# Row maxima of self-attention as pairs of 64-row products, and scores in two single PSUM banks

## The chip, the cores and the metric

One NeuronCore of a Trainium2 (trn2) chip. The metric is the device time of one execution in microseconds, the median of several runs. PE is TensorE's matmul side, PEld its weight loads, DVE VectorE, ACT ScalarE, POOL GpSimd, SP the engine that issues most DMAs.

## What is computed

x is (2, 1024, 256). It is layer-normed and put through a conditioned transformer block; the result is added to x and goes through a quantised feed-forward. Cut to what matters here:

```python
h1 = adaln(x, t, norm1_w, norm1_b)
x = mha(h1, h1, attn1_wq, ...) + x          # 16 heads of 64, 1024 keys
h2 = adaln(x, t, norm2_w, norm2_b)
x = mha(h2, context, attn2_wq, ...) + x     # 77 keys
x = glu_ff(adaln(x, t, norm3_w, norm3_b), ...) + x
# mha: scores = q @ k.T / 8 ; attn = softmax(scores) ; out = attn @ v ; out @ wo + bo
```

The change is in the softmax of mha: its row maxima and its scores.

## The kernel before

**Units.** Self-attention runs over 16 units: 2 batches x 8 pairs of heads. In each unit both heads get q, k and v (items of PE that ACT and DVE split into a high and a low f16 part), maxima, scores, exps, the exps' low parts ("rest"), values, and two transposes of the result ("out"). Pieces of later work fill in: in units 0 to 3 the norms of the second batch, in units 4 to 7 and 12 to 15 two tiles of an output projection ("projA"), in units 8 to 11 two others and norms ("projB", "norm").

**Operands.** SP's `restack` copies q and k by DMA into `head_operands` (`HB`): per head four planes QS, QM, KH, KL of 128 rows. Rows 0 to 63 of QS hold the high part of q and rows 64 to 127 its low part; KH holds the high part of k in both halves.

**Maxima.** softmax needs the row maximum of the scores before the exps, because exps are taken of scores laid out with keys on the partitions; there the negated maximum comes in as one row of the product (row 64 of QM). A "max" item is one product of 128 rows, (q high + q low) x k high, 128 queries by 512 keys, one bank. There are 32 a unit (head, 8 query tiles, 2 halves of the keys), 512 in all. They alternate between the two banks of `mixed` (`M_[0]`, `M_[1]`). DVE reduces each (L1842), and after the last of a head reduces the pairs into `neg_max` (L1854); PE transposes that ("row", L870), ACT copies it and issues the DMA that puts it into row 64.

**Scores, exps, rest, values.** A unit has 16 chunks: head, half of the queries, group of 256 keys. A chunk of scores is four products of 512 columns (L904, L905, twice) into `scores{c % 2}`, a pair of banks; ACT takes one exp of 128 x 1024 (L1248); POOL (DVE for chunk 14) makes the low parts (L1574, L1869); values are 24 small products (L927 to L929) into `PV_[0]`. `exps` is a ring of four chunks. q, k, v, out, projections and norms take the bank `PV_[1]` in turn: each waits until ACT and DVE have emptied it.

**Order.** The order of a unit is written out by hand (FIRST_UNIT, SELF_UNIT; the last unit by a generic loop, `unit`). PE runs it as it stands; ACT, POOL and DVE run the same list with small shifts by kind (SELF_LAGS). Every engine works strictly in its order, so a wait holds all that stands behind it. The tail of SELF_UNIT before is

```python
("max", 1, 1, 5), ("values", 15), ("max", 1, 1, 6), ("max", 1, 1, 7), ("slot", 15), ("out", 0, 1), ("slot", 16)
```

The first number of a max, q, k, v, row or out says whether it is of this unit (0) or the next (1); "slot" marks only places for rare notes. In a unit the maxima of head 1 end early and those of the next unit's head 0 and half of its head 1 follow.

## Time and profile before

| | us |
|---|---|
| median of 3 runs | 1193.1 (1189.34 to 1197.38) |
| the profiled execution | 1193.03 |
| its span, first to last instruction | 1191.2 |
| PE busy | 1101.7 |
| DVE busy | 859.7 |
| POOL busy | 694.4 |
| ACT busy | 591.2 |

The span begins with the first instruction and ends with the last; 1.8 us of the execution lie outside. Self-attention runs from about 50 to 790 us, cross-attention to about 1000, the feed-forward to the end. A busy time is the sum of the listed durations with overlaps counted once. A view of waits says for whom an engine stood idle; the chain follows the work that ended last back in time.

### The profile page before, as it was taken

The numbers are of one execution on the slowest core, as the hardware profiler recorded it, in microseconds if no ns is written. First come the engines' busy times: TensorE is split into PE (matmuls) and PEld (weight loads), VectorE is DVE, ScalarE is ACT, GpSimd is POOL, SyncE is SP. The second block draws the span as 40 slices with busy tenths as digits, with TensorE's granted clock in tenths as the row PEclk, the third lists the DMA queues.
The fourth block names the chain that finished last, engine by engine and source line by source line (L and its number), as shares of the span: only waits on it lengthen the run. The fifth ranks groups of instructions, "written<-read, shape, count | busy, mean of one in ns | idle before, by whom it ended". The sixth has DMA issues, their size and how long they took to land.

```text
span 1191.2 us, 30646 instructions
## 1 busy us (share of the span) xinstructions
PE 1101.7 (92%) x12733; PEld 720.2 (60%) x12740; DVE 859.7 (72%) x1686; ACT 591.2 (50%) x856; POOL 694.4 (58%) x641
## 2 busy tenths in 40 slices
PE   4799999999999999999999999889899989999995
PEld 1355665665656656657656566567667666656663
DVE  6687767756657668678676676848867976887887
ACT  4444455444444444444444445544444544258668
POOL 5757766765656657777676556436534743533333
PEclk9899999999999999999999999999999999999999
DMA  8420220220220211202202203122432444000001
GB/s 288 118 61 2 55 55 1 55 55 2 55 54 2 55 28 28 55 2 55 55 2 55 54 2 90 37 59 59 131 85 60 87 103 152 1 1 10 10 18 36
DMA packets 41854, 63.52 MB, mean 53 GB/s; under 512 B 11459, under 2 KB 22383, under 8 KB 41461
## 3 DMA queue, kind: packets, MB, share of 16 engines
q1 hardware_dynamic: 40413, 60.91, 20.4%
q8 instruction: 101, 1.65, 0.6%
q10 hardware_dynamic: 1304, 0.66, 0.2%
q14 instruction: 36, 0.29, 0.1%
HBM read 20.63 MB, written 2.10 MB: 19 GB/s over the span
## 4 chain that ended last, share of the span: by engine, by line
PE 68%; DVE 16%; ACT 5%; DMA 4%; issue 4%; POOL 2%; SPq 0%; ACTq 0%; DVEq 0%
PE outs L839 9%; PE scores L904 8%; PE scores L905 7%; PE mixed L860 6%; PE outs L816 6%; PE scores L966 5%; PE outs L929 4%; PE outs L927 4%; DVE maxes L1842 4%; PE outs L928 4%; PE outs L980 4%; PE outs L849 3%; DMA head_operands<-neg_max_rows 3%; DVE exps_rest L1869 2%; PE outs L877 2%
## 5 line engine op out<-in xcount | busy, mean ns | idle before, releaser
L1574 POOL TENSOR_TENSOR exps_rest<-exps 128x1024 f16<-128x1024 f32 (+1 forms) x297 | 510.8, 1725 | 305.8 <-ACT exps L1248 304.8
L1248 ACT ACTIVATE exps<-scores 128x1024 f32<-128x1024 f32 (+1 forms) x320 | 297.1, 938 | 261.9 <-PE scores L905 242.1
L1842 DVE TENSOR_REDUCE maxes<-mixed 128x1 f32<-128x512 f32 x512 | 334.6, 683 | 90.9 <-PE mixed L860 86.4
L927 PE MATMUL outs<-values,exps 128*128 128x65 f16 (+1 forms) x2176 | 226.7, 193 | 1.8 <-POOL exps_rest L1574 1.7
L928 PE MATMUL outs<-values,exps 128*128 128x64 f16 (+1 forms) x2176 | 226.7, 192 | 0.0
L929 PE MATMUL outs<-values,exps_rest 128*128 128x65 f16 (+1 forms) x2176 | 226.4, 194 | 0.0
L904 PE MATMUL scores<-head_operands 128*128 128x512 f16 (+1 forms) x576 | 218.6, 380 | 6.9 <-DMA head_operands<-neg_max_rows 6.6
L905 PE MATMUL scores<-head_operands 128*128 128x512 f16 (+1 forms) x576 | 218.5, 379 | 0.0
L927 PEld LDWEIGHTS outs<-values,exps 128*128 128x128 bf16 (+1 forms) x2176 | 201.6, 98 | 22.3 <-POOL exps_rest L1574 3.4
L928 PEld LDWEIGHTS outs<-values,exps 128*128 128x128 bf16 (+1 forms) x2176 | 200.6, 98 | 23.4
L929 PEld LDWEIGHTS outs<-values,exps_rest 128*128 128x128 f16 (+1 forms) x2176 | 200.5, 97 | 0.0
L860 PE MATMUL mixed<-head_operands 128*128 128x512 f16 x512 | 178.0, 385 | 16.9 <-DVE maxes L1842 10.0
L839 PE MATMUL outs<-hT,weights 128*128 128x512 f16 x492 | 120.7, 382 | 3.4 <-DVE qk_pairs L1827 2.4
L1827 DVE SCALAR_TENSOR_TENSOR qk_pairs<-outs,qk_pairs 128x512 f16<-128x512 f32 x82 | 56.4, 688 | 77.7 <-ACT qk_pairs L1213 77.7
L860 PEld LDWEIGHTS mixed<-head_operands 128*128 128x128 f16 x512 | 48.7, 97 | 76.4 <-DVE maxes L1842 34.8
L816 PE MATMUL outs<-weights,attn_outT 128*128 128x256 f16 x744 | 92.0, 274 | 0.0
L904 PEld LDWEIGHTS scores<-head_operands 128*128 128x128 f16 (+1 forms) x576 | 57.4, 100 | 49.4 <-issue 8.8
L905 PEld LDWEIGHTS scores<-head_operands 128*128 128x128 f16 (+1 forms) x576 | 57.6, 100 | 49.0
L966 PE MATMUL scores<-hT,weights 128*128 128x512 f16 x384 | 86.8, 379 | 0.0
L1213 ACT ACTIVATE qk_pairs<-outs 128x512 f16<-128x512 f32 x82 | 49.0, 597 | 68.2 <-PE outs L839 66.6
L816 PEld LDWEIGHTS outs<-weights,attn_outT 128*128 128x128 f16 x744 | 71.4, 98 | 11.2
L839 PEld LDWEIGHTS outs<-hT,weights 128*128 128x128 f16 x492 | 43.9, 98 | 54.7 <-DVE attn_outT L1862 7.8
(204 smaller groups left out, 1576.9 us busy)
## 6 DMA issues: line engine op xcount, KB each, us to landing
head_operands<-qk_pairs SPq DMA_DIRECT2D x128, 256.0 KB, 4.4
head_operands<-qk_pairs SPq DMA_DIRECT2D x32, 128.0 KB, 2.4
stage<-in_L_xcond_ff_w_dram SPq DMA_DIRECT2D x3, 1024.0 KB, 5.0
residual<-in_x_dram SPq DMA_DIRECT2D x4, 512.0 KB, 10.0
stage<-in_L_ffn_w_dram SPq DMA_DIRECT2D x2, 1024.0 KB, 5.0
head_operands<-in_x_dram SPq DMA_DIRECT2D x1, 2048.0 KB, 9.4
out_dram<-out_tile SPq DMA_DIRECT2D x16, 128.0 KB, 1.7
attn_outT<-in_L_xcond_attn_wq_dram SPq DMA_DIRECT2D x1, 1024.0 KB, 8.6
```

Source lines behind the costliest of these rows:

```text
L816: last = mm(ITEM[bank][:, 0:D], OT[:, c, xh, t * P:(t + 1) * P], W[:, 3, wh, c * D:(c + 1) * D], start=(n_ == 0 and c == 4 * half), stop=( ...
L839: last = mm(m[:, 0:rhs.shape[-1]], W[:, 0 if kind == "q" else 1, wh, wc[c]], rhs, start=(n_ == 0 and c == 0), stop=(n_ == 2 and c == KC - 1))
L860: last = mm(m[:, :], hb[:, QS, t * P:(t + 1) * P], hb[:, KH, kh * HALF:(kh + 1) * HALF], start=True, stop=True)
L904: mm(o, kb[:, KH, :], hb[:, QS, :], start=True, stop=False)
L905: last = mm(o, kb[:, KL, :], hb[:, QM, :], start=False, stop=True)
L927: mm(o, eb[:, sl], vb[:, DH:VW], start=(kt == 0 and q == 0), stop=False, skip_group_check=True)
L928: mm(o[:, 0:DH], eb[:, sl], vb[:, 0:DH], start=False, stop=False, skip_group_check=True)
L929: last = mm(o, R[0:a.ks, slot, sl], vb[:, DH:VW], start=False, stop=(kt == a.kt - 1), skip_group_check=True)
L966: last = mm(SP_[f % 2][:, half * HALF:(half + 1) * HALF], WU[:, wh, k, half * F + f * P:half * F + (f + 1) * P], hT[:, xh, k, tc * HALF:(t ...
L1248: A(E[0:a.ks, c % RING, 0:n], SP_[c % 2][0:a.ks, 0:n], ACT.Exp, scale=SCALE).then_inc(s.exps, 1)
L1574: G.tensor_tensor(R[0:a.ks, c % RING, 0:n], e, e.bitcast(BF16).rearrange("p (n two) -> p n two", two=2)[:, :, 1], ALU.subtract).then_inc(s ...
L1842: V.tensor_reduce(mx[:, h, t, kh:kh + 1], m[:, :], AX_X, ALU.max).then_inc(s.maxed, 1)
```

## The change

Maxima. A max item now covers one query tile and all 1024 keys as two products of 64 rows each: high q by high k, keys 0 to 511 from rows 0 to 63 of the array, keys 512 to 1023 from rows 64 to 127. For the second, a new tile `query_copies` (QD) holds the high part of q in rows 64 to 127; a fourth DMA of `restack` fills it, behind a wait of SP for the maxima of the previous unit's same head. The item fills two banks: even tiles both banks of `mixed`, odd tiles both banks of `scores1`. The written orders always name two items together, a visit of four products into four banks. DVE reduces 128 x 1024 at once and straight into the negated maximum, so `maxes` and L1854 go. There are 16 items, 8 visits, a unit. (The low part of q no longer enters the maximum, which only has to lie near the true one.)

Scores. `scores0` alone is left: a chunk becomes two parts ("scores", 2c + j) with one bank and one exp of 128 x 512 each. A part waits for the exp two parts before it. In cross-attention banks and products stay.

Orders. The three self-attention orders are written anew with 32 parts of scores and 8 visits a unit, the last unit has one of its own (LAST_UNIT), and `unit` and `extras` go. The set-up's transposes ("columns") go to `PV_[1]`, and `outb` is laid into `head_operands`.

```diff
+    def exps(self, g, c, j=0):
+        return self.kpc * (self.chunks * g + c) + j + 1
+    SHARED = {5: (3,), 6: (0, 1)}
     def add(self, kind, ai=0, g=0, what=None, c=None, bank=None):
...
+            if ai == 0 and what[0] == "max":
+                bank = 5 if what[2] % 2 else 6
...
+        ITEM = [M_[0], M_[1], PV_[1][:, :], SP_[1][:, HALF:2 * HALF], PV_[0][:, :], SP_[1][:, :], MM[:, :]]
+        def score_bank(a, c, j):
+            if a.kt == 1:
+                return SP_[c % 2][0:a.ks, 0:HALF]
+            return SP_[0][:, j * HALF:(j + 1) * HALF]
...
                     if ai == 0:
                         moves += [(hb[0:DH, KH:KL + 1, :], ST[rows, K_HI:K_LO + 1, :]),
-                                  (hb[DH:P, QS:KH + 1:KH - QS, :], ST[rows, Q_LO:K_HI + 1, :])]
+                                  (hb[DH:P, QS:KH + 1:KH - QS, :], ST[rows, Q_LO:K_HI + 1, :]),
+                                  (QD[DH:P, h, :], ST[rows, Q_HI, :])]
+                        if g:
+                            sp.wait_ge(s.maxed, a.max_items * (2 * g - 1 + h))
...
                     if ai == 0:
-                        last = mm(m[:, :], hb[:, QS, t * P:(t + 1) * P], hb[:, KH, kh * HALF:(kh + 1) * HALF],
-                                  start=True, stop=True)
+                        q = slice(t * P, (t + 1) * P)
+                        mm(m[:, 0:HALF], hb[0:DH, QS, q], hb[0:DH, KH, 0:HALF], start=True, stop=True)
+                        last = mm(m[:, HALF:2 * HALF], QD[DH:P, h, q], hb[DH:P, KH, HALF:2 * HALF], start=True, stop=True)
...
-                before = a.chunks * g + c - 1
+                j = part or 0
+                before = a.exps(g, c, j) - 2
...
                 elif before > 0:
                     pe.wait_ge(s.exps, CREDIT + before)
...
-                for j in range(a.kpc):
-                    k0 = (gr * a.kpc + j) * P
-                    kb = HB[:, par, h, :, k0:k0 + a.ks]
-                    o = SP_[c % 2][0:a.ks, j * HALF:(j + 1) * HALF]
-                    mm(o, kb[:, KH, :], hb[:, QS, :], start=True, stop=False)
-                    last = mm(o, kb[:, KL, :], hb[:, QM, :], start=False, stop=True)
-                last.then_inc(s.scores, 1)
+                k0 = (gr * a.kpc + j) * P
+                kb = HB[:, par, h, :, k0:k0 + a.ks]
+                o = score_bank(a, c, j)
+                mm(o, kb[:, KH, :], hb[:, QS, :], start=True, stop=False)
+                mm(o, kb[:, KL, :], hb[:, QM, :], start=False, stop=True).then_inc(s.scores, 1)
...
-                n = a.kpc * HALF
-                A(E[0:a.ks, c % RING, 0:n], SP_[c % 2][0:a.ks, 0:n], ACT.Exp, scale=SCALE).then_inc(s.exps, 1)
+                A(E[0:a.ks, c % RING, j * HALF:(j + 1) * HALF], score_bank(a, c, j), ACT.Exp, scale=SCALE).then_inc(s.exps, 1)
...
-                        V.tensor_reduce(mx[:, h, t, kh:kh + 1], m[:, :], AX_X, ALU.max).then_inc(s.maxed, 1)
+                        V.tensor_reduce(nm[:, h, t:t + 1], m[:, :], AX_X, ALU.max, negate=True).then_inc(s.maxed, 1)
```

The new order of a unit, as the later steps name it:

```python
SELF_UNIT = (
    ("scores", 2), ("rest", 0), ("scores", 3), ("q", 1, 0), ("max", 0, 1, 4), ("max", 0, 1, 5), ("slot", 0),
    ("rest", 1), ("scores", 4), ("values", 0), ("scores", 5), ("rest", 2), ("q", 1, 1), ("scores", 6), ("slot", 1),
    ("scores", 7), ("slot", 2), ("values", 1), ("k", 1, 0), ("scores", 8), ("scores", 9), ("scores", 10),
    ("k", 1, 1), ("scores", 11), ("rest", 3), ("values", 2), ("rest", 4), ("max", 0, 1, 6), ("max", 0, 1, 7),
    ("rest", 5), ("scores", 12), ("norm1", 0), ("scores", 13), ("slot", 3), ("projB", 0), ("rest", 6),
    ("values", 3), ("row", 0, 1), ("rest", 7), ("v", 1, 0), ("slot", 4), ("scores", 14), ("slot", 5), ("values", 4),
    ("scores", 15), ("normT1", 0), ("values", 5), ("values", 6), ("scores", 16), ("max", 1, 0, 0), ("max", 1, 0, 1),
    ("norm", 0), ("scores", 17), ("hi1", 0), ("slot", 6), ("v", 1, 1), ("scores", 18), ("rest", 8), ("scores", 19),
    ("values", 7), ("normT", 0), ("slot", 7), ("projA", 0), ("max", 1, 0, 2), ("max", 1, 0, 3), ("lo1", 0),
    ("slot", 8), ("rest", 9), ("norm1", 1), ("hi", 0), ("scores", 20), ("values", 8), ("scores", 21), ("rest", 10),
    ("lo", 0), ("scores", 22), ("hi1", 1), ("scores", 23), ("max", 1, 0, 4), ("max", 1, 0, 5), ("projB", 1),
    ("slot", 9), ("values", 9), ("normT1", 1), ("scores", 24), ("rest", 11), ("scores", 25), ("slot", 10),
    ("projA", 1), ("lo1", 1), ("values", 10), ("max", 1, 0, 6), ("max", 1, 0, 7), ("norm", 1), ("rest", 12),
    ("values", 11), ("normT", 1), ("hi", 1), ("slot", 11), ("slot", 12), ("scores", 26), ("scores", 27),
    ("scores", 28), ("slot", 13), ("rest", 13), ("scores", 29), ("row", 1, 0), ("values", 12), ("lo", 1),
    ("rest", 14), ("max", 1, 1, 0), ("max", 1, 1, 1), ("scores", 30), ("values", 13), ("rest", 15), ("scores", 31),
    ("slot", 14), ("out", 0, 0), ("scores", 32), ("scores", 33), ("values", 14), ("max", 1, 1, 2), ("max", 1, 1, 3),
    ("values", 15), ("slot", 15), ("out", 0, 1), ("slot", 16))
```

## Rows read from the trace of the kernel before

**Rows 1.** The page: span, busy time, granted clock by slice, chain by engine.

```profile
PE 1101.7 (92%) x12733; PEld 720.2 (60%) x12740; DVE 859.7 (72%) x1686; ACT 591.2 (50%) x856; POOL 694.4 (58%) x641
...
PEclk9899999999999999999999999999999999999999
...
PE 68%; DVE 16%; ACT 5%; DMA 4%; issue 4%; POOL 2%; SPq 0%; ACTq 0%; DVEq 0%
```

**Rows 2.** Timeline (start us, duration us, engine, line, count): 512-column products.

```profile
501.90 0.38 PE L904 MATMUL scores<-head_operands 128*128 128x512 f16 x1
...
502.12 0.38 PE L905 MATMUL scores<-head_operands 128*128 128x512 f16 x1
...
502.34 0.38 PE L860 MATMUL mixed<-head_operands 128*128 128x512 f16 x1
```

**Rows 3.** Timeline: values products with weight loads; twelve of a projection.

```profile
500.34 0.19 PE L929 MATMUL outs<-values,exps_rest 128*128 128x65 f16 x1
...
500.37 0.19 PE L927 MATMUL outs<-values,exps 128*128 128x65 f16 x1
...
505.06 1.47 PE L816 MATMUL outs<-weights,attn_outT 128*128 128x256 f16 x12
```

**Rows 4.** Windows of two units: us, busy PE PEld DVE ACT POOL, PEclk, DMA.

```profile
302.43:349.06 46.63, 45.07 (x587) 29.37 (x588) 31.05 (x54) 21.48 (x26) 28.39 (x16) 1.00 0.16 35
538.10:584.70 46.60, 45.56 (x595) 29.82 (x592) 33.54 (x64) 21.97 (x28) 33.16 (x24) 1.00 0.15 35
```

**Rows 5.** Waits of PE and PEld, 100:700: total us, times, longest us.

```profile
PE mixed L870 <- DVE neg_max L1854: 6.1, 9, 0.7
PE outs L877 <- DVE attn_out L1882: 5.0, 13, 0.4
PE mixed L860 <- DVE maxes L1842: 4.5, 12, 0.4
PE mixed L860 <- DMA head_operands<-qk_pairs: 2.1, 2, 1.1
...
PEld mixed L860 <- DVE maxes L1842: 19.8, 52, 0.7
```

**Rows 6.** Timeline at the set-up transposes: v, 2-row, 16-row and 77-row products.

```profile
51.63 0.50 PE L849 MATMUL outs<-weights,hT 128*128 128x128 f16 x6
...
52.06 0.65 PE L771 MATMUL scores<-identf,exps_rest 2*128 2x2 f32 x8
...
52.58 0.21 PE L791 MATMUL scores<-identf,exps 16*128 16x16 f32 x1
...
52.72 0.49 PE L795 MATMUL scores<-identf,stage 77*128 77x77 f32 x4
```

**Rows 7.** Groups with shapes apart: count, busy us, mean ns, idle before.

```profile
L1842 DVE TENSOR_REDUCE maxes<-mixed 128x1 f32<-128x512 f32 x512 | 334.6, 683 | 90.9 <-PE mixed L860 86.4 <-PE mixed L870 0.7
...
L1213 ACT ACTIVATE qk_pairs<-outs 128x512 f16<-128x512 f32 x82 | 49.0, 597 | 68.2 <-PE outs L839 66.6 <-DMA head_operands<-qk_pairs 1.0
...
L1844 DVE TENSOR_REDUCE maxes<-mixed 128x4 f32<-128x308 f32 x64 | 28.8, 471 | 4.3 <-PE mixed L865 3.5
...
502.80 1.87 DVE L1842 TENSOR_REDUCE maxes<-mixed 128x1 f32<-128x512 f32 x3
```

**Rows 8.** Timeline, then chain, at values 15, out and the next q.

```profile
612.46 0.19 PE L927 MATMUL outs<-values,exps 128*128 128x65 f16 x1
...
613.18 0.61 PE L860 MATMUL mixed<-head_operands 128*128 128x512 f16 x2
...
614.17 0.63 PE L877 MATMUL outs<-identf,attn_out 128*128 128x128 f32 x4 [0.38 <-DVE attn_out L1882]
...
613.60 0.43 DVE attn_out L1882
...
616.22 1.47 PE outs L839 x6
```

**Rows 9.** The page: DMA issues of q and k copies, KB, us to landing.

```profile
head_operands<-qk_pairs SPq DMA_DIRECT2D x128, 256.0 KB, 4.4
```

More of the change, by code:

```diff
@@ L60 @@
 FIRST_UNIT = (
-    ("max", 0, 0, 0), ("max", 0, 0, 1), ("max", 0, 0, 2), ("max", 0, 0, 3), ("max", 0, 0, 4), ("max", 0, 0, 5),
-    ("max", 0, 0, 6), ("max", 0, 0, 7), ("max", 0, 0, 8), ("setup", "rows"), ("v", 0, 0), ("first", 0, 0),
-    ("max", 0, 0, 9), ("v", 0, 1), ("setup", "columns"), ("max", 0, 0, 10), ("max", 0, 0, 11), ("scores", 0),
-    ("rest", 0), ("max", 0, 0, 12), ("scores", 1), ("max", 0, 0, 13), ("max", 0, 0, 14), ("q", 1, 0),
-    ("scores", 2), ("max", 0, 0, 15), ("max", 0, 1, 0), ("rest", 1), ("values", 0), ("q", 1, 1), ("rest", 2),
@@ new lines @@
+    ("max", 0, 0, 0), ("max", 0, 0, 1), ("max", 0, 0, 2), ("max", 0, 0, 3), ("setup", "rows"), ("v", 0, 0),
+    ("first", 0, 0), ("max", 0, 0, 4), ("max", 0, 0, 5), ("v", 0, 1), ("setup", "columns"), ("scores", 0),
+    ("rest", 0), ("scores", 1), ("scores", 2), ("max", 0, 0, 6), ("max", 0, 0, 7), ("scores", 3), ("q", 1, 0),
+    ("scores", 4), ("scores", 5), ("rest", 1), ("values", 0), ("q", 1, 1), ("rest", 2), ("row", 0, 0),
+    ("max", 0, 1, 0), ("max", 0, 1, 1), ("scores", 6), ("values", 1), ("scores", 7), ("k", 1, 0),
@@ L187, in add @@
             bank = self.bank(kind == "normT" and len(self.outer_banks) > 1)
-        step = Step(kind, ai, g, what, c, bank, self.last.get(bank), self.items[ai])
+        banks = self.SHARED.get(bank, (bank,))
+        after = []
+        for k in banks:
+            if self.last.get(k) not in (None, *after):
+                after.append(self.last[k])
+        step = Step(kind, ai, g, what, c, bank, after, self.items[ai])
         if bank is not None:
-            self.last[bank] = step
+            for k in banks:
+                self.last[k] = step
         self.steps.append(step)
@@ L242, in self_unit @@
             if kind == "setup":
-                self.add("setup", what=at[0])
+                self.add("setup", what=at[0], bank=2 if at[0] == "columns" else None)
+            elif kind == "cross":
+                self.add("item", 1, at[0], tuple(at[1:]))
             elif (g, kind, at[0]) == (0, "v", 0):
                 self.add("item", 0, 0, (kind, at[1]), bank=(2, 4)[at[1]])
-            elif kind in ("scores", "rest", "values"):
+            elif kind == "scores":
+                c = at[0] // a.kpc
+                self.add(kind, 0, g + c // a.chunks, at[0] % a.kpc, c % a.chunks)
+            elif kind in ("rest", "values"):
                 self.add(kind, 0, g + at[0] // a.chunks, c=at[0] % a.chunks)
@@ L942, in piece @@
                 elif st.kind == "scores":
[L943 removed]
+                    scores(st.ai, st.g, st.c, st.what)
                 elif st.kind == "values":
@@ L1253, in piece @@
                 elif st.kind == "scores":
-                    exps(st.ai, st.g, st.c)
+                    exps(st.ai, st.g, st.c, st.what)
                 elif st.kind == "split":
```

251 lines of the change are left out of this document (79 added, 172 removed).

## The prediction

> **What bounds the kernel now.** I read the page first. PE is busy 92% of the span and holds 68% of the chain that ended last, DVE 16%, and the granted clock is full nearly everywhere, its upper level of 2.4 GHz [rows 1]. That busy share alone decides nothing, because ends of matmuls are modelled and overlap. So I went to the timeline and read starts. A 512-column matmul is listed with 0.38 us, but the next one starts 0.215 to 0.22 us later [rows 2]. Product and weight load of a values matmul start every 0.03 us [rows 3]. By such steps I count one unit (one pair of heads) of self-attention: maxima 32 x 0.216 = 6.9 us, scores 64 x 0.216 = 13.8, values 384 x 0.0303 = 11.7, q and k 24 x 0.216 = 5.2, v 48 x 0.056 = 2.7, projections 24 x 0.11 = 2.6, transposes 1.1; together 44.0 us. The unit takes 46.6 us, from the first row transpose of one to that of the next, in the two kinds of stage that I looked at [rows 4]. PE's issue of products therefore bounds self-attention, and some 2.6 us a unit are waits. The view of waits of 12.9 units (100 to 700 us) says for whom: DVE's maxima, neg_max and attn_out above all [rows 5]. ACT is busy 21.5 us and POOL 28 to 33 us of the 46.6 us, DVE 31 to 33.5 [rows 4]. So a saved column of PE counts in full, and a late DVE or ACT counts as soon as the written order gives PE nothing in front of it.
>
> **Part 1, the products of the maxima.** 512 matmuls of 128 rows become 512 of 64 rows in 256 pairs. If the two of a pair stream side by side, a pair costs 0.216 us; if one after the other, 0.432, what the two cost today [rows 2]. No row before shows two halves working at once. I take the near end, plus one step of 0.03 us a visit for the second product's own weight load and issue [rows 3], because the two halves share neither rows of the array nor a bank. The Trainium skill (TensorE: Matmul & The Clock Gate, Part 3, Measured speedup) has four such tiles at 3.07 times, which by itself would put a pair nearer the side-by-side end too; no run shown yet bears on it.
>
> **Part 2, switching the array's shape.** A visit is entered from and left to 128-row work, so each visit has two switches. The only rows like it are at 52 us: the first 2-row transposes begin 0.15 us after the last product of v (51.63 plus five steps of 0.056 is 51.91), where 0.056 would do, and the first 77-row transpose begins 0.14 us after the 16-row one, where the eight 2-row ones before it came 0.06 us apart, and nothing is waited for [rows 6]. That is 0.09 and 0.08 us; with a weight load that can't be fetched ahead I take 0.1; below, nothing (a shape change might hide under streaming); above, the 0.16 us by which a product's listed time exceeds its step [rows 2]. A visit then costs 0.1 + 0.03 + 2 x 0.216 + 0.1 = 0.66 us for what cost 4 x 0.216 = 0.86. Eight visits: 5.3 against 6.9, **-1.6 us a unit** (-2.9 to -0.7). The skill (TensorEngine Tiling (Array Packing), Key Properties) says that changing the tiling mode drains TensorE, a rule against this change; rows 6 agree with it, and its page gives no price.
>
> **Part 3, DVE.** A reduce of 308 elements takes 471 ns, one of 512 takes 683, so 1.04 ns an element; one of 1024 is about 1.2 us, and two back to back 1.15 + 1.2 = 2.35 us [rows 7]. Per unit DVE falls by about 32 x 0.63 + 2 x 0.17 - 16 x 1.15 = 2.2 us, which is worth nothing by itself, since DVE is not the bound. But a visit now leaves DVE a block of 2.35 us that nothing can pass, where it was one, two or three times 0.62.
>
> That block falls on the worst place. The new order ends a unit with values 14, maxima (1,1,2) and (1,1,3), values 15, out (0,1), and DVE keeps that order. Before, values 15 were issued from 612.46 to 613.18, DVE took them at once (rden, then attn_out until 614.03), PE filled 0.43 us with two maxima, and out's transposes began at 614.17; the following q began 2.05 us after them, at 616.22 [rows 8]. After: call the visit's start 0. Its first product ends at 0.1 + 0.38, DVE starts its reduces at 0.53 and is free at 2.9; rden and attn_out until 3.5; out at 3.6. PE is ready at 0.66 + 0.73 = 1.4, so it waits 2.2 us. Then out (0.44), scores 2 and 3 (0.86), and q waits for out's two copies until 3.6 + 2.05 = 5.65, 0.75 us more. Sum of waits 2.95; before, from 612.46 to 616.22 are 3.76 us with 2.9 of work (0.73 + 0.43 + 0.44 + 0.22 + 0.86 + 0.22), some 0.8 us of waits. **+2.15 us a unit.** What is late next: nothing, the maxima that follow (0,1,4) come 1.3 us later on free banks.
>
> **Part 4, scores in two single banks.** A part (two products, 0.43 us) may start when the exp two parts back is done. An exp of 512 columns takes 0.59 to 0.60 us as an ACT copy of this size does [rows 7]. From a part's start to the end of its exp: 0.216 + 0.38 + 0.05 + 0.6 = 1.25 us. In a run of three parts with nothing between, the third is ready after 0.86 and waits 0.4. The new order has three such runs: 8, 9, 10 right behind k, whose copy (0.60) ACT does first: 0.55 us; 21, 22, 23: 0.4; 26 to 29: 0.4 and 0.15. Today chunks of four products have two banks each and the timeline has no such wait. **+1.5 us a unit**; 0 if ACT is never met, 2.5 if its other copies fall in each. ACT does 512 exps in place of 256; even at a whole 0.2 us more a chunk that is 3.2 us a unit beside 21.5 of 46.6 [rows 4]: hidden.
>
> **Part 5, waits that go.** PE's waits for maxima before L860: 4.5 us by the PE rows and 19.8 by the weight loads, of which part is covered by streaming; I take 12 us in 12.9 units. Visits now lie 3.4 to 5 us apart against a block of 2.35: **-0.95 us**. The transpose of a row behind the last maxima waits up to 0.7 us in one of two places today [rows 5]. The second row of a unit now has 3 us ahead of it, the first has only scores 12, 13 and values 3 behind the visit (1.6 us against 3.1) and waits 0.85, save in the four units with a projection between: **-0.2**. Scores 32 wait for the row's copy and DMA and come 3.4 us of work after its transpose, where it was 3.6: **+0.1**.
>
> **Part 6, the rest.** One more DMA a head (32 of 128 KB; now 4.4 us to landing) behind a wait on SP for the previous unit's maxima. Behind it on SP are only this head's own copies and the weight reloads; the maxima that need them start 5 us later (head 0) and 20 us (head 1); PE waited 2.1 us for these copies in all [rows 5, 9]. Nothing. If that cover failed it would be one landing, some 4 us, a unit. Cross-attention and feed-forward keep their products, exps and banks; `outb` only changes its address. The set-up's transposes move to another bank, once: below 1 us.
>
> **Sum.** -1.6 + 2.15 + 1.5 - 0.95 - 0.2 + 0.1 = +1.0 us, times 15 units = +15. The last unit has a written order with values between all parts and no visit at its end, so only part 2 stays of the terms: -1. The profiled execution took 1193.03 us, which is the median of the three (1193.1). 1193 + 15 - 1 = **1207 us**.
>
> **Rivals.**
> *The switch is free.* 256 switches (16 units x 8 x 2) x 0.1 = 26 us less: 1181 us, not slower. For it: of two switches seen, one has a semaphore wait on it and both are 4-byte transposes. Against it: the second had no wait. It decides below 0.05 us a switch. 0.17. By the skill's rule on draining (page above) this case would not come.
> *The wait before out does not come*, because DVE reaches values 15 before the second reduce, or PE gets there later than I think: 2.15 x 15 = 32 us less, 1175 us. Against it: DVE's program follows the same list, and today's chain runs over just this place [rows 8]. 0.12.
> *The pairs do not overlap*: the change does not do what it says. A pair costs 0.432 us, 256 x 0.19 = 48 us more: 1255 us. Nothing in the trace excludes it. 0.13.
> *The forecast*, 1195 to 1220 us by the half of each term that is unsure: 0.48; the remaining 0.10 are mixtures, as much on either side.
>
> About 1% is what a measurement of this kernel can tell from no change: 1181 to 1205. Slower: six tenths of the forecast, all of the pairs' case, a little of the mixtures: 0.45. Faster: the out case, four tenths of the free switch, some mixtures: 0.23. Within 1%: 0.32. Leaving out the pairs' case and the lower half of the out case gives 1176 to 1240 us.
>
> **What would show it.** Starts of the four products of a visit: pairs within some 0.03 us, pair to pair 0.216; 0.43 if they don't overlap. The start of the first product against the one before it, and of what follows: 0.1 us beyond the step. Reduces of 1024: 1.2 us, DVE's group of maxima some 300 us in 256 instead of 335 in 512. In the view of waits: PE (or its weight loads) at out's transposes for attn_out, some 30 us more; a new wait of scores L904 for ACT's exps, 20 us or more; the wait of L860 for maxima nearly gone. A unit from row to row: 47.6 us. I am wrong if out's wait stays below 1 us, or if a visit takes under 0.5 us from its first start to the next work's.

## The result and the profile after

The changed kernel takes 1232.6 us (median of four, 1230.8 to 1236.7) against 1195.2 us for the kernel before on the same chip (median of four: the three runs above and one more): 1.032 times as long, interval 1.027 to 1.038. It is 37 us slower, where 14 were forecast. The profiled execution took 1236.65 us with a span of 1234.6, so the two profiled spans differ by 43.4 us, and this is the sum to be explained by the trace.

The page of the kernel after: busy time by engine, granted clock in 40 slices, chain by engine.

```profile
PE 1097.7 (89%) x12740; PEld 690.3 (56%) x12740; DVE 829.8 (67%) x1365; ACT 607.4 (49%) x1112; POOL 697.7 (57%) x641
...
PEclk7699999999999999999999999999999998999998
...
PE 66%; DVE 16%; ACT 6%; issue 4%; POOL 4%; DMA 3%; SPq 1%; ACTq 0%; DVEq 0%; POOLq 0%
```

PE is busy 4 us less than in [rows 1] and the span is 43 us longer, so PE has no more work than before and stands idle for 47 us more. The line of the clock shows that the start ran at a lower clock than before. Kernel after, waits of PE, then of its weight loads, 100 to 700 us (total us, times, longest us), as [rows 5] for before:

```profile
PE outs L837 <- DVE attn_out L1829: 22.8, 12, 2.0
PE scores L863 <- ACT exps L1205: 10.2, 37, 0.3
PE outs L761 <- DVE normed L1705: 7.2, 4, 1.8
PE mixed L830 <- DVE neg_max L1801: 5.0, 8, 0.6
PE outs L798 <- DVE attn_outT L1809: 5.0, 9, 0.6
```

```profile
PEld scores L863 <- ACT exps L1205: 39.5, 68, 0.8
```

Out's transposes (now L837) wait 22.8 us where they waited 5.0; scores (L863) wait for exps, which had no row before; q and k (L798) wait for the copies of out's result (attn_outT, L1809); and norm's transposes (L761), of which the prediction had said nothing, wait four times 1.8 us. The maxima no longer wait for DVE.

The same stretches in both traces, cut at the transposes of head 1's row in units 1, 4, 8, 12 and 14 (from : to, length, busy PE PEld DVE ACT POOL, granted clock, DMA). Two more follow in the text. Kernel before:

```profile
0.00:121.10 121.10, 93.14 (x867) 50.01 (x867) 86.63 (x179) 55.82 (x75) 80.72 (x96) 0.96 0.39 117
121.10:255.80 134.70, 129.50 (x1698) 82.94 (x1699) 93.99 (x166) 68.24 (x89) 96.58 (x61) 1.00 0.16 37
255.80:444.40 188.60, 181.74 (x2357) 118.74 (x2358) 124.61 (x213) 85.93 (x104) 114.02 (x61) 1.00 0.16 36
444.40:630.90 186.50, 181.52 (x2353) 118.51 (x2350) 133.96 (x253) 87.89 (x112) 132.35 (x93) 1.00 0.16 35
630.90:725.40 94.50, 90.31 (x1173) 58.83 (x1174) 62.12 (x107) 42.96 (x52) 56.76 (x31) 1.00 0.16 35
```

Kernel after:

```profile
0.00:134.30 134.30, 95.32 (x868) 47.97 (x869) 87.14 (x143) 57.40 (x98) 81.90 (x97) 0.85 0.36 110
134.30:274.00 139.70, 127.21 (x1698) 75.73 (x1698) 88.39 (x111) 71.08 (x137) 95.78 (x61) 0.98 0.18 41
274.00:466.60 192.60, 178.02 (x2357) 109.99 (x2358) 115.32 (x141) 89.85 (x168) 113.73 (x61) 0.98 0.18 41
466.60:671.50 204.90, 181.28 (x2353) 111.51 (x2350) 125.98 (x181) 92.41 (x176) 132.73 (x93) 0.97 0.17 37
671.50:766.50 95.00, 86.96 (x1173) 53.82 (x1174) 57.46 (x71) 44.71 (x84) 56.59 (x31) 1.00 0.18 41
```

Start to unit 1: +13.2 us. Units 1 to 4: +5.0. 4 to 8: +4.0. 8 to 12, the ones with norms: +18.4. 12 to 14: +0.5. From there to the first row's transpose of cross-attention +3.1 (64.2 to 67.3 us), all that follows -0.8. Two of these differences are smaller than what the change costs there: in the kernel before PE waited 1.01 us (until 354.0) and 1.10 us (until 635.9) for the copies of q and k, the 2.1 us of [rows 5], and the kernel after has no such wait over 0.2 us. Without them 4 to 8 is +5.0 and 12 to 14 is +1.6. Two things stand out. The loss is far from even over the units, so it can't be one wait in each. And the granted clock, 1.00 before, is 0.97 or 0.98 where most of the loss is, and 1.00 in units 12 and 13, where it is small.

Kernel after, timeline of a visit (start us, duration us, engine, line, tiles):

```profile
502.27 1.47 PE L798 MATMUL outs<-hT,weights 128*128 128x512 f16 x6 [0.55 <-DVE attn_outT L1809]
...
503.67 0.39 PE L820 MATMUL mixed<-head_operands 64*128 64x512 f16 x1
503.67 0.39 PE L821 MATMUL mixed<-head_operands,query_copies 64*128 64x512 f16 x1
...
503.89 0.38 PE L820 MATMUL scores<-head_operands 64*128 64x512 f16 x1
503.90 0.38 PE L821 MATMUL scores<-head_operands,query_copies 64*128 64x512 f16 x1
...
504.20 0.39 PE L863 MATMUL scores<-head_operands 128*128 128x512 f16 x1
```

The two products of a pair start within 0.01 us, the pairs 0.22 us apart. Six products of q at 0.216 end their turn at 502.27 + 1.30 = 503.57, so the entry costs 0.10; from the second pair to the next work are 0.31 us, 0.09 beyond the step. The visit takes 0.63 us, with 0.66 forecast.

Kernel after, timeline at the end of a unit (values 15 issued from 497.44 to 498.16):

```profile
497.18 1.23 DVE L1801 TENSOR_REDUCE neg_max<-mixed 128x1 f32<-128x1024 f32 x1 [0.55 <-PE mixed L821]
...
498.32 1.21 DVE L1801 TENSOR_REDUCE neg_max<-scores 128x1 f32<-128x1024 f32 x1
499.45 0.17 DVE L1827 RECIPROCAL rden<-outs 128x4 f32<-128x4 f32 x1
499.65 0.42 DVE L1829 TENSOR_TENSOR attn_out<-outs,rden 128x256 f32<-128x256 f32 x1
...
500.22 0.63 PE L837 MATMUL outs<-identf,attn_out 128*128 128x128 f32 x4 [1.87 <-DVE attn_out L1829]
```

This is the block of the prediction's Part 3, in its place and size: two reduces, 2.35 us, then rden and attn_out, and PE idle for about 2 us. The row of q at 502.27 above carries the rest, 0.55 us of waiting for attn_outT (0.7 us from start to start).

### The profile page after: what moved, and what is told of

Same layout as the page of the kernel before. It is cut to its first block, busy times and chain, and to the rows that moved or that the text cites. A ratio compares the mean times of both kernels' runs of the same rounds, so it can differ in the third digit from the quotient of the medians.

```text
span 1234.6 us, 30607 instructions
## 1 busy us (share of the span) xinstructions
PE 1097.7 (89%) x12740; PEld 690.3 (56%) x12740; DVE 829.8 (67%) x1365; ACT 607.4 (49%) x1112; POOL 697.7 (57%) x641
## 4 chain that ended last, share of the span: by engine, by line
PE 66%; DVE 16%; ACT 6%; issue 4%; POOL 4%; DMA 3%; SPq 1%; ACTq 0%; DVEq 0%; POOLq 0%
PE outs L798 9%; PE scores L863 8%; DVE neg_max L1801 7%; PE scores L864 7%; PE outs L775 5%; PE scores L924 5%; PE outs L885 4%; PE outs L887 4%; PE outs L886 4%; PE outs L938 3%; PE outs L808 3%; PE mixed L820 3%; ACT exps L1205 2%; POOL exps_rest L1531 2%; PE outs L837 2%
## 5 line engine op out<-in xcount | busy, mean ns | idle before, releaser
L1205 ACT ACTIVATE exps<-scores 128x512 f32<-128x512 f32 (+1 forms) x576 | 325.9, 596 | 254.5 <-PE scores L864 233.0
L863 PE MATMUL scores<-head_operands 128*128 128x512 f16 (+1 forms) x576 | 225.2, 391 | 16.2 <-ACT exps L1205 12.7
L885 PE MATMUL outs<-values,exps 128*128 128x65 f16 (+1 forms) x2176 | 230.4, 194 | 7.8 <-POOL exps_rest L1531 5.6
L885 PEld LDWEIGHTS outs<-values,exps 128*128 128x128 bf16 (+1 forms) x2176 | 202.7, 99 | 53.5 <-POOL exps_rest L1531 22.6
L886 PE MATMUL outs<-values,exps 128*128 128x64 f16 (+1 forms) x2176 | 229.8, 193 | 0.0
L887 PE MATMUL outs<-values,exps_rest 128*128 128x65 f16 (+1 forms) x2176 | 229.2, 195 | 0.0
L864 PE MATMUL scores<-head_operands 128*128 128x512 f16 (+1 forms) x576 | 223.8, 388 | 0.0
L1801 DVE TENSOR_REDUCE neg_max<-mixed 128x1 f32<-128x1024 f32 x128 | 156.1, 1220 | 77.6 <-PE mixed L821 77.5
L1801 DVE TENSOR_REDUCE neg_max<-scores 128x1 f32<-128x1024 f32 x128 | 155.2, 1213 | 0.0
L798 PE MATMUL outs<-hT,weights 128*128 128x512 f16 x492 | 127.5, 398 | 13.0 <-DVE qk_pairs L1784 6.9
L863 PEld LDWEIGHTS scores<-head_operands 128*128 128x128 f16 (+1 forms) x576 | 57.9, 100 | 107.9 <-ACT exps L1205 51.2
L798 PEld LDWEIGHTS outs<-hT,weights 128*128 128x128 f16 x492 | 46.3, 101 | 72.7 <-DVE attn_outT L1809 13.3
L1196 ACT ACTIVATE attn_outT<-outs 128x512 f16<-128x512 f32 x49 | 29.1, 596 | 75.0 <-PE outs L837 74.8
```

Source lines behind the costliest of these rows:

```text
L798: last = mm(m[:, 0:rhs.shape[-1]], W[:, 0 if kind == "q" else 1, wh, wc[c]], rhs, start=(n_ == 0 and c == 0), stop=(n_ == 2 and c == KC - 1))
L863: mm(o, kb[:, KH, :], hb[:, QS, :], start=True, stop=False)
L864: mm(o, kb[:, KL, :], hb[:, QM, :], start=False, stop=True).then_inc(s.scores, 1)
L885: mm(o, eb[:, sl], vb[:, DH:VW], start=(kt == 0 and q == 0), stop=False, skip_group_check=True)
L886: mm(o[:, 0:DH], eb[:, sl], vb[:, 0:DH], start=False, stop=False, skip_group_check=True)
L887: last = mm(o, R[0:a.ks, slot, sl], vb[:, DH:VW], start=False, stop=(kt == a.kt - 1), skip_group_check=True)
```

## The experiments

All were compared with the kernel before on the same chip (its medians there are 1195 to 1197 us). The changed kernel itself comes first once more, with no edit:

> The changed kernel as it is, for comparison on this chip. Expected 1230 to 1237 us with a granted clock of 0.96 to 0.98, ratio 1.03 to the kernel before. If the lower clock were an accident of the first executions, it would read 0.99 here and about 1215 us.

1233.6 us, 1.030 times before (1.025 to 1.035), as expected, so the lower clock is no accident of the first executions.

**pairs_serial and rows128: are the pairs and the switches as read?** The first makes the second product of a pair use the same 64 rows as the first, so the two can't run at once:

```diff
-  last = mm(m[:, HALF:2 * HALF], QD[DH:P, h, q], hb[DH:P, KH, HALF:2 * HALF], start=True, stop=True)
+  last = mm(m[:, HALF:2 * HALF], hb[0:DH, QS, q], hb[0:DH, KH, HALF:2 * HALF], start=True, stop=True)
```

> Both products of an item take rows 0 to 63 of the array, so that they must go one after the other; the same products, banks, reduces and switches. My theory (the pairs stream side by side and save 0.2 us each, the loss lies in waits): 256 x 0.2 = 50 us more, a little less where PE waits anyway, 1270 to 1285 us, and a visit of about 0.95 us from first start to the next work's. The rival, that the pairs bring nothing: unchanged, 1233 us.

The second makes both of 128 rows, with the high and low part of q as before, so there is no switch either:

```diff
-  mm(m[:, 0:HALF], hb[0:DH, QS, q], hb[0:DH, KH, 0:HALF], start=True, stop=True)
-  last = mm(m[:, HALF:2 * HALF], QD[DH:P, h, q], hb[DH:P, KH, HALF:2 * HALF], start=True, stop=True)
+  mm(m[:, 0:HALF], hb[:, QS, q], hb[:, KH, 0:HALF], start=True, stop=True)
+  last = mm(m[:, HALF:2 * HALF], hb[:, QS, q], hb[:, KH, HALF:2 * HALF], start=True, stop=True)
```

> The two products of an item are again of 128 rows (q high and low), one after the other, but in the new order and banks: no change of the array's shape, no overlap. My theory, with a switch at 0.1 us: 50 us more for the pairs and 26 less for 256 switches, 1250 to 1260 us. The rival, that a switch costs nothing: the same as the serial pairs, 1280 us. The rival, that pairs and switches together are what lost the time: below the changed kernel, 1200 us.

1269.7 us and 1251.1 us, the first at the low edge of what was expected and the second within it; after_again, in the same comparison, 1233.6. Serial pairs cost 36 us, 128-row products 17.5. The two kernels differ by 18.6 us and by the 256 switches, so at most 0.07 us each. It is not a clean price, since the stretches at half clock, of which more below, differ too: there are 13 and 6 of them between 100 and 800 us, and at some 1 us for each the switches are left with about 0.05 us (an estimate). The timeline of pairs_serial at a visit's last product and the next work:

```profile
514.70 0.38 PE L821 MATMUL scores<-head_operands 64*128 64x512 f16 x1
515.01 0.39 PE L863 MATMUL scores<-head_operands 128*128 128x512 f16 x1
```

The same place in rows128:

```profile
515.53 0.38 PE L821 MATMUL scores<-head_operands 128*128 128x512 f16 x1
515.74 0.38 PE L863 MATMUL scores<-head_operands 128*128 128x512 f16 x1
```

0.31 us against 0.21: leaving 64-row work costs 0.1 us, and it is the shape that costs it. Parts 1 and 2 of the prediction hold, and pairs are better than either serial form: the loss lies elsewhere.

**half_reduce and before_half: is it DVE's block?** DVE reduces half of the columns, in the kernel after and in the kernel before. Both leave work out, since the maximum is then over half of the keys:

```diff
-  V.tensor_reduce(nm[:, h, t:t + 1], m[:, :], AX_X, ALU.max, negate=True).then_inc(s.maxed, 1)
+  V.tensor_reduce(nm[:, h, t:t + 1], m[:, 0:HALF], AX_X, ALU.max, negate=True).then_inc(s.maxed, 1)
...
-  V.tensor_reduce(mx[:, h, t, kh:kh + 1], m[:, :], AX_X, ALU.max).then_inc(s.maxed, 1)
+  V.tensor_reduce(mx[:, h, t, kh:kh + 1], m[:, 0:HALF // 2], AX_X, ALU.max).then_inc(s.maxed, 1)
```

> DVE reduces only the first 512 of the 1024 columns (the maximum is taken over half the keys, which leaves work out); everything else stays. My theory, DVE's block of 2.4 us ahead of values 15 and of the norms: the block falls to 1.3 us, out's wait from 1.9 to about 0.9 us, the norms' too, and the half-clock stretches that follow these waits go: 1195 to 1205 us. The rival, that the scores' single banks behind ACT are the loss: 1225 to 1233 us.

> The kernel before with each of its 512 reduces over 256 of the 512 columns (maximum over half the keys, leaves work out): what the length of DVE's reduces is worth there. My theory, that short blocks between other work cost PE little: the 1 us a unit of waits for maxima and half of that for rows, 1180 to 1188 us. The rival, that DVE's total work is what bounds a unit in either kernel: as much as in the changed kernel, 45 us, 1150 us.

half_reduce: 1188.7 us, 0.994 times before (0.991 to 0.996), 45 us under after_again and more than the 29 to 39 us expected. before_half: 1183.1 us, 0.988 times before (0.983 to 0.993), as expected, only some 14 us under its own base. A reduce takes 0.68 us in place of 1.22 in the first and 0.42 in place of 0.68 in the second, so both save DVE about the same time in all. The length of the reduces costs three times as much in the new order as in the old one. With the reduces halved in both, 5 to 7 us are left of the change's 37. Waits of PE in half_reduce, 100 to 700 us:

```profile
PE outs L837 <- DVE attn_out L1829: 11.0, 13, 1.0
...
PE outs L761 <- DVE normed L1705: 3.0, 4, 0.7
```

Out waits 12 us less and norm's transposes 4 less. Over all of self-attention that is some 20 us, far short of 45; where more of it lies, in the clock, is shown further down.

**end_visit: the wait before out alone.** The last visit of a unit goes to the start of the next, and the one after it moves back, so that no maxima stand ahead of values 15:

```diff
-    ("scores", 2), ("rest", 0), ("scores", 3), ("q", 1, 0), ("max", 0, 1, 4), ("max", 0, 1, 5), ("slot", 0),
+    ("scores", 2), ("rest", 0), ("scores", 3), ("max", 0, 1, 2), ("max", 0, 1, 3), ("q", 1, 0), ("slot", 0),
...
-    ("scores", 7), ("slot", 2), ("values", 1), ("k", 1, 0), ("scores", 8), ("scores", 9), ("scores", 10),
+    ("scores", 7), ("slot", 2), ("max", 0, 1, 4), ("max", 0, 1, 5), ("values", 1), ("k", 1, 0), ("scores", 8),
...
-    ("slot", 14), ("out", 0, 0), ("scores", 32), ("scores", 33), ("values", 14), ("max", 1, 1, 2), ("max", 1, 1, 3),
-    ("values", 15), ("slot", 15), ("out", 0, 1), ("slot", 16))
+    ("slot", 14), ("out", 0, 0), ("scores", 32), ("scores", 33), ("values", 14),
+    ("values", 15), ("slot", 15), ("out", 0, 1), ("slot", 16))
```

(The first and the last unit follow suit.)

> Only the place of one visit: maxima (1,1,2) and (1,1,3) go from ahead of values 15 to the start of the next unit, behind scores 3, and (0,1,4) and (0,1,5) behind scores 7. My theory: out's wait falls from 1.9 to 0.5 us and q's behind it from 0.6 to nothing, and the half-clock stretches of 3.4 us behind them go: 2 us a unit and 1.5 more in eight units, 1190 to 1203 us. The rival, that the scores' banks are the loss: within 5 us of the changed kernel. The rival, that the block only finds another victim: above 1215 us.

1214.9 us, 1.017 times before (1.012 to 1.022): some 18 us won where 31 to 44 were expected, and hardly under the 1215 us above which the expectation saw the block only find another victim. Waits of PE, 100 to 700 us:

```profile
PE outs L885 <- POOL exps_rest L1531: 11.1, 19, 0.7
PE outs L837 <- DVE attn_out L1829: 10.7, 13, 0.8
```

Out's wait fell by 12 us, and that of q for attn_outT (5.0) went. But values (L885) came earlier than POOL had their low parts: 11.1 us against 3.1. POOL had been hidden by the wait that was taken away. In these rows the balance is 12 + 5 - 8 = 9 us won; the other half of the 18 is not in these waits.

**norm_visit: norm's transposes alone.** The visit ahead of them goes behind them:

```diff
-    ("projA", 1), ("lo1", 1), ("values", 10), ("max", 1, 0, 6), ("max", 1, 0, 7), ("norm", 1), ("rest", 12),
-    ("values", 11), ("normT", 1), ("hi", 1), ("slot", 11), ("slot", 12), ("scores", 26), ("scores", 27),
+    ("projA", 1), ("lo1", 1), ("values", 10), ("norm", 1), ("rest", 12),
+    ("values", 11), ("normT", 1), ("hi", 1), ("max", 1, 0, 6), ("max", 1, 0, 7), ("slot", 11), ("slot", 12),
```

> Only the visit (1,0,6) and (1,0,7) goes from ahead of the norm's statistics to behind its transposes, which exist in units 8 to 11 alone. My theory: in these four units 2 us of wait for DVE go and perhaps a half-clock stretch, in the others the row behind waits up to 0.8 us more: 1220 to 1232 us, with units 8 to 11 at 48 to 49 us in place of 51.2. If these units are long for another cause, they stay at 51 us.

1232.8 us (1225.6 to 1237.8), just above the 1220 to 1232 expected: no change that can be told from the scatter. The wait of norm's transposes is nearly gone (7.2 us in the kernel after), and the transpose of the row, which follows the visit sooner now in every unit, waits more (5.0 us there):

```profile
PE mixed L829 <- DVE neg_max L1800: 8.2, 20, 0.6
...
PE outs L760 <- DVE normed L1704: 1.1, 4, 0.3
```

(One line fewer in this kernel, so L829 is L830 of after.) The move helps in four units (units 8 to 11 take some 49 us in place of 51), and the row's longer wait takes back 3.2 us in these rows. Why nothing at all is left of it in the median is not shown.

**short_exp: the scores' waits for exps.** From unit 1 on an exp takes half of its columns, which leaves that work out:

```diff
-  A(E[0:a.ks, c % RING, j * HALF:(j + 1) * HALF], score_bank(a, c, j), ACT.Exp, scale=SCALE).then_inc(s.exps, 1)
+  w = HALF // 2 if ai == 0 and g else HALF
+  A(E[0:a.ks, c % RING, j * HALF:j * HALF + w], score_bank(a, c, j)[:, 0:w], ACT.Exp, scale=SCALE).then_inc(s.exps, 1)
```

> The changed kernel with self-attention's exps over 256 of the 512 columns of a part, from the second unit on (leaves that work out; the low parts and values read what stood in the tile). An exp falls from 0.60 to about 0.33 us, so a third part in a run waits 0.1 in place of 0.4 us. My step on the single banks (1.5 us a unit): 15 to 20 us less, 1213 to 1219 us. The rival, that these waits overlap with waits for DVE: 1226 us or more. The rival, that ACT's latency also sets POOL's low parts and so the values: below 1205 us.

1226.7 us, 7 us under the kernel after, where 15 to 20 were expected. The waits of scores for exps leave PE's list and fall from 39.5 to 29.3 us in that of the weight loads, but out's wait grew to 26.5 us (22.8). Of a wait that PE has ahead of a later, longer one a part would have been waited there anyway. The kernel also has 11 stretches at half clock between 100 and 790 us, where the kernel after has 8, which hides up to some 5 us more of gain.

**runs_broken: the runs of scores split.** Scores 10, scores 23 and values 12 each move by one to three items of PE, to break the three runs of Part 4:

```diff
-    ("scores", 8), ("scores", 9), ("scores", 10), ("k", 1, 1),
+    ("scores", 8), ("scores", 9), ("k", 1, 1), ("scores", 10),
...
-    ("scores", 22), ("hi1", 1), ("scores", 23), ("max", 1, 0, 4), ("max", 1, 0, 5),
+    ("scores", 22), ("hi1", 1), ("max", 1, 0, 4), ("max", 1, 0, 5), ("scores", 23),
...
-    ("scores", 27), ("scores", 28), ("slot", 13), ("rest", 13), ("scores", 29), ("row", 1, 0), ("values", 12),
+    ("scores", 27), ("values", 12), ("scores", 28), ("slot", 13), ("rest", 13), ("scores", 29), ("row", 1, 0),
```

> Only the three runs of score parts are broken: 10 goes behind k, 23 behind a visit, values 12 between 27 and 28. My theory: 1.3 us a unit, 1210 to 1218 us, and the wait of scores for exps falls to a third. The rival, that the single banks are the main loss: below 1200 us. The rival, that PE's wait just moves to the next thing: 1228 us or more.

1261.6 us: 28 us slower than the kernel after, where a gain of 15 to 24 was expected. Waits of PE, 100 to 700 us:

```profile
PE outs L797 <- DVE qk_pairs L1783: 9.7, 12, 3.6
...
PE outs L884 <- DVE attn_out L1828: 7.7, 7, 1.2
PE outs L884 <- POOL exps_rest L1530: 7.6, 10, 1.3
...
PE scores L862 <- ACT exps L1204: 5.3, 5, 1.7
```

The waits for exps halved, as they should. But scores 10 had given DVE the time to empty the bank of k's first half; without it k's second half waits 0.55 us in every unit (and in one place, at 129 us, 3.6 us where the kernel after has 2.7). And values 12, now earlier, waits for attn_out of values 11, which on DVE stands behind the maxima (1, 0, 6) and (1, 0, 7). At least two of the three runs were no oversight in the order: they covered other waits with a shorter one.

**reorder, reorder2, reorder3: a version without these places.** reorder has all three moves above, and also (0, 1, 6) and (0, 1, 7) ahead of k's second half and scores 33 between values 15 and out:

> All three moves together, (0,1,6) and (0,1,7) ahead of the second k, and score part 33 between values 15 and out. My theory adds up: 1170 to 1185 us, below the kernel before, with the clock at 0.98 or more. If DVE or POOL is the real bound of a unit, it stays above 1195 us.

1206.0 us, 1.010 times before (1.006 to 1.013), 20 to 35 us above the expectation. Waits of PE, 100 to 700 us:

```profile
PE outs L885 <- POOL exps_rest L1531: 19.4, 25, 1.1
...
PE outs L837 <- DVE attn_out L1829: 5.6, 13, 0.8
```

Out waits 17 us less, values wait 16 more for POOL: a later part of scores gives a later exp and a later low part. reorder2 spreads the last parts of scores between the other items and takes values 14 behind the first out:

```diff
-    ("row", 1, 0), ("lo", 1), ("rest", 14), ("max", 1, 1, 0), ("max", 1, 1, 1), ("scores", 30), ("values", 13),
-    ("rest", 15), ("scores", 31), ("slot", 14), ("out", 0, 0), ("scores", 32), ("values", 14),
-    ("values", 15), ("slot", 15), ("scores", 33), ("out", 0, 1), ("slot", 16))
+    ("row", 1, 0), ("lo", 1), ("rest", 14), ("scores", 30), ("max", 1, 1, 0), ("max", 1, 1, 1), ("scores", 31),
+    ("values", 13), ("rest", 15), ("slot", 14), ("out", 0, 0), ("values", 14), ("scores", 32), ("scores", 33),
+    ("values", 15), ("slot", 15), ("out", 0, 1), ("slot", 16))
```

> The reordered kernel with its two largest waits addressed: maxima (1,1,0) and (1,1,1) one score part behind the row, whose copy holds the same bank (0.9 us a unit), and score part 31 ahead of values 13 with values 15 last, so that POOL's low parts for values 15 are done (1.2 us a unit). My theory that only places are wrong: some 1.5 us a unit less than the reordered kernel, 1180 to 1192 us, ratio 0.99 to the kernel before. If each block of 2.35 us of DVE finds another victim wherever it stands: 1200 us or more.

1195.0 us, 1.000 (0.997 to 1.002), 3 us above the 1180 to 1192 expected: values' wait for POOL is down to 7.4 us, units take 44 to 47 us. What stayed were single waits of 2 to 4 us in the first, second and last unit. reorder3 mends most of them (the first piece below is of FIRST_UNIT, the second of LAST_UNIT, and the note at slot 2 of SELF_UNIT moves behind scores 10):

```diff
-    ("max", 0, 1, 3), ("rest", 4), ("k", 1, 1), ("scores", 10), ("max", 0, 1, 4), ("max", 0, 1, 5), ("scores", 11),
-    ("scores", 12), ("norm1", 0), ("rest", 5), ("scores", 13), ("scores", 14), ("max", 0, 1, 6), ("max", 0, 1, 7),
+    ("max", 0, 1, 3), ("rest", 4), ("scores", 10), ("scores", 11), ("k", 1, 1), ("scores", 12), ("max", 0, 1, 4),
+    ("max", 0, 1, 5), ("norm1", 0), ("rest", 5), ("scores", 13), ("scores", 14), ("max", 0, 1, 6), ("max", 0, 1, 7),
...
-    ("scores", 12), ("rest", 5), ("row", 0, 1), ("scores", 13), ("values", 4), ("projA", 0),
+    ("scores", 12), ("rest", 5), ("scores", 13), ("values", 4), ("row", 0, 1), ("projA", 0),
...
-            return c not in SELF_RESTS if g < UNITS - 1 else bool(c % 2)
+            return c not in SELF_RESTS if g < UNITS - 1 else c < 6 or bool(c % 2)
```

> The second reordered kernel with three one-off places mended, all outside the repeated unit: in the last unit POOL makes the low parts of chunks 0, 2 and 4 in DVE's place and the row stands one values later (waits of 3.0, 2.1 and 3.8 us there); in the first unit two score parts ahead of the second k (2.4 us); in the second unit the token statistics behind the maxima (2.1 and 0.9 us). My theory, that the time lost at the ends of self-attention has the same cause, a late DVE: 6 to 9 us less, 1186 to 1190 us, ratio 0.992 to 0.995 to the kernel before. If these waits only cover others: 1195 us, ratio 1.

1186.2 us, as expected, and 0.993 times before (0.991 to 0.994): 9 us faster than the kernel before on its chip, and some 46 faster than the change as it was made. Its products, reduces and exps are those of the change, and but for three low parts of the last unit (chunks 0, 2 and 4), which went from DVE to POOL, only the order differs. Waits of PE, 100 to 700 us:

```profile
PE outs L837 <- DVE attn_out L1829: 10.7, 13, 0.8
PE outs L885 <- POOL exps_rest L1531: 7.5, 13, 0.7
```

No wait of 2 us is left in these 600 us, and the granted clock is halved there once, at 193 us. The kernel before was not given a new order, so the 9 us do not say what the new operations would be worth against the old ones in an order as carefully made.

## Why the prediction was right in direction and too small in size

1232.6 us lies above the 1195 to 1220 us of the forecast itself. It is inside 1176 to 1240 us only because that took in the mixtures, which had a chance of 0.10.

**Parts 1 and 2, right.** Pairs side by side, 0.10 and 0.09 us a switch by the timeline, at most 0.07 by two kernels. The 3.07 times that Part 1 quotes is for tiles of 32 rows, so it is the starts within 0.01 us that show it for 64. (The low end of Part 2's range does not follow from its terms: without any price for the switch it is -3.2 us a unit, not -2.9.) The two rivals that hung on them fall: pairs do overlap (the forced serial form costs 36 us more), and the switch is not free, since it costs 0.09 us or more in the timeline. The Trainium skill (TensorEngine Tiling (Array Packing), Key Properties) says that changing the mode drains TensorE; the 0.31 us against 0.21 behind the last product agree.

**Part 3, right for out, and incomplete.** Block 2.35 us, wait about 2 us against 2.2 forecast, q's wait 0.55 by the view and 0.7 from start to start against 0.75. "Wrong if out's wait stays below 1 us" did not come. Kernel after, one of the two groups of reduces (count, busy us, mean ns):

```profile
L1801 DVE TENSOR_REDUCE neg_max<-mixed 128x1 f32<-128x1024 f32 x128 | 156.1, 1220 | 77.6 <-PE mixed L821 77.5
```

With the 128 of the other banks (155.2 us) that is 311 us in 256 instead of 335 in 512 [rows 7], with 300 forecast. The step that failed is the list behind it. The prediction asked who waits for DVE behind one visit, the last of the unit, and called it the worst place. In units 8 to 11 the visit (1, 0, 6) and (1, 0, 7) stands ahead of norm on DVE, and norm's transposes wait there by the same block, about 2 us, four times: 8 us that the sum did not have. The same question, asked at each of the eight visits, would have found it.

**Part 4, seen as waits, not as time.** Start to start, the runs of scores stall PE by about 20 us in 100 to 800 us, 1.4 us a unit, and 1.5 was the term. Yet halving the exps, which by this term should have given 15 to 20 us, gave back 7 us in all, about 0.5 us a unit, and no more than 0.8 with the clock allowed for. The term was added as if nothing followed it, though out's wait for a fixed chain on DVE follows it in the same unit.

**Part 5, right in the row that could be checked.** The wait of the maxima for DVE, 4.5 us by PE's rows and 19.8 by the weight loads, no longer appears. The row's transpose waits 5.0 us against 6.1.

**Part 6, the set-up and first unit, wrong.** The fourth DMA cost nothing, as forecast: PE waits 0.2 us for query_copies between 100 and 700 us (in reorder3 it is 5.7 us). But the part had "below 1 us" for the set-up, and for the first unit nothing but the terms of the repeated one; the first stretch grew by 13.2 us. The first row's transpose starts at 61.04 us before, at 67.36 after, and at 62.06 in norm_visit, whose order up to there is that of after. So some 5 us are the start-up's clock, which differs between executions of the same order, 1 us is the change, and 6.9 us (60.1 to 66.9 us) lie between that row and unit 1's. Kernel after, waits of PE from 50 to 134.3 us:

```profile
PE outs L798 <- DVE qk_pairs L1784: 4.9, 2, 2.7
PE outs L808 <- POOL weights L1506: 2.1, 1, 2.1
```

Before, the list of this stretch has 0.7 us for qk_pairs and nothing for the weights. FIRST_UNIT is an order of its own and should have been walked through like SELF_UNIT. That the last unit gives back 1 us can't be checked: the stretch behind it is 0.8 us shorter, which is within what executions differ by.

**What was not in the sum at all: the clock.** Kernel after, three windows in unit 8:

```profile
485.80:489.20 3.40, 1.37 (x7) 0.67 (x8) 2.87 (x7) 0.75 (x2) 1.70 (x2) 1.00 0.00 0
489.20:492.60 3.40, 3.40 (x31) 2.02 (x32) 0.99 (x1) 1.98 (x5) 3.40 (x3) 0.50 0.00 0
492.60:496.00 3.40, 3.40 (x43) 2.00 (x40) 2.80 (x4) 1.78 (x4) 1.46 (x2) 1.00 0.02 5
```

In the first, PE is busy for 1.37 of 3.40 us, because norm's transposes wait. Then the granted clock is 0.50, the 1.2 GHz level, while PE has work without a gap, and then full again. The timeline of PE there:

```profile
487.57 0.41 PE L761 MATMUL outs<-identf,normed 128*128 128x128 f32 x2 [1.80 <-DVE normed L1705]
...
489.45 0.63 PE L864 MATMUL scores<-head_operands 128*128 128x512 f16 x1
489.88 0.63 PE L863 MATMUL scores<-head_operands 128*128 128x512 f16 x1
```

The products start 0.43 us apart in place of 0.216. Such stretches of some 3.4 us begin in the kernel after at 209.3, 257.1, 304.9, 352.7, 489.2, 540.4, 591.6 and 642.8 us: two in units 1 to 4, two in 4 to 8, four in 8 to 12, none in 12 to 14, which is how the granted clock fell in the rows from 0 to 766.5 us above. The kernel before has none in self-attention after its start. All eight stand beside a wait: out's ended at 209.4, 255.7, 304.5 and 353.0 us, norm's at 487.6, 538.8, 590.0 and 641.3, so each stretch begins between 0.3 us before the end of a wait of about 2 us and 1.6 us after it. Not every such wait is followed by one: between 100 and 700 us there are 12 of out's and 4 of norm's for eight stretches.

The other kernels bear the link out. In all profiled executions together there are 66 such stretches between 100 and 790 us, and each begins near the end of a wait of PE of 1.6 us or more (0.7 us before it to 2.6 us after it); out's waits of 0.8 us in end_visit and half_reduce are followed by none. With out's wait cut (end_visit), the four stretches between 200 and 360 us are gone and, from 200 to 790 us, two are left, at 528.5 and 579.5 us, where waits of norm's end at 528.4 and 578.4. That fits the half of end_visit's gain that its waits did not show. With norm's wait cut (norm_visit), two are left between 480 and 650 us, both behind a wait of out's. But norm_visit has none between 200 and 360 us either, though out waits 1.87 or 1.88 us there, and 1.87 to 1.92 in the kernel after. So a wait of this length makes a stretch possible and not certain, and the number of stretches is no clean measure of an edit. With the block halved (half_reduce) there is none from 130 to 790 us.

What a stretch costs can be read where units of one kind run with it and without. Kernel end_visit, from the row of head 1 in unit 8 to that in unit 9, without a stretch, and from there to unit 10, with one:

```profile
458.60:507.40 48.80, 44.17 (x596) 27.17 (x593) 32.18 (x46) 22.76 (x44) 33.32 (x24) 1.00 0.18 39
507.40:557.40 50.00, 45.62 (x596) 27.56 (x593) 31.52 (x46) 23.04 (x44) 33.33 (x24) 0.97 0.17 38
```

The next two take 50.1 us with a stretch and 48.3 without, so it costs 1.2 to 1.8 us there. In the kernel after, units without norms take 48.3 and 48.5 us with one and 47.5 to 48.1 without: 0.2 to 1.0 us. The most that it can cost is 1.7 us, half of 3.4, to within what units differ by; where PE would have waited next, it costs less. For the eight, four of each kind, that makes some 6 to 11 us, an estimate.

**The sum again.** Of 43.4 us between the profiled spans, 13.2 are the first stretch (5 of them the start-up's clock), 8 norm's waits, some 6 to 11 the clock. The 11 to 16 us left are what the terms of the prediction answer for, with its 14. Units 12 and 13, at full clock and without norms, took 47.5 us each, and 47.6 was forecast; before they took 47.9, of which 1.1 is the wait for the copies, and 46.6. So the part of the loss that was forecast came out about as large as forecast. That is luck in part, since Part 4's term was worth 0.5 to 0.8 in place of 1.5 and what made up for it is not settled. The error of the forecast is in three places that were not looked at: the first unit, norm's waits and the clock. The median, 37 us, is 6 less than the profiled pair, since both profiled executions of the changed kernel (1236.65 and 1237.3 us, mean granted clock 0.963 and 0.960) are the longest of theirs (the others have 0.968 to 0.978).

How much each of norm's wait, the clock and the first unit takes of the median is not settled: norm_visit took the first away and its median did not move. That the length of DVE's block is behind most of it is shown by half_reduce beside before_half.

## What to carry to other kernels

Merging small operations into one long one makes a block that nothing can pass: go through every place of the written order where it falls, in the first and the special stages too, and write down who on the critical engine waits behind it. Don't add waits of one unit that lie ahead of a longer wait; the later one absorbs them, and taking a short wait away can uncover a longer one (runs_broken, +28 us) or the engine behind it (end_visit, POOL). Judge a change of operations and the order around it apart: here the new operations came out 9 us ahead of the old kernel once their order fitted them, and 37 behind it with the order that came with them.

## What the runs showed of the hardware

- Two products of 64 rows in different halves of the array, 128 x 512 each into two banks, start within 0.01 us and take 0.22 us from pair to pair; on the same half, 0.21 each in turn.
- From 64-row to 128-row work: 0.09 to 0.10 us beyond the step in the timeline, and 0.10 us for entering 64-row work.
- A DVE reduce of 128 x 1024 from two banks takes 1.22 us, two back to back 2.35 us.
- A wait of PE of 1.6 to 2.7 us can be followed by a stretch of 3.4 us at the 1.2 GHz level in which the products take twice their step (0.43 us in place of 0.216); in the kernel after 8 of 19 such waits between 100 and 790 us were. A stretch lengthened a unit by 0.2 to 1.8 us. PE's clock is therefore a cost of waits, even in a kernel that is busy 89% of its span.
- The clock in the first 60 us differs between executions of the same order, by some 5 us of time at the first row's transpose.
